# A decoder layer on one core: another bank and another sender for the first pair, feed-forward weights scaled by GpSimd, bounds in three operations

## The reference, cut to what matters

```python
x = layernorm(x + self_attention(x))          # q, k, v with biases, wo, bo
x = layernorm(x + cross_attention(ctx, ctx, x))  # 8x8 weights shared by all heads
x = layernorm(x + ffn(x))

def qlinear(x, W, b):            # ffn: qlinear, exact gelu, qlinear; 128 -> 512 -> 128
    amin, amax = min(x), max(x)                      # over the whole tensor
    scale = maximum((amax - amin) / 255, 1e-8)
    zp = clip(round(-amin / scale) - 128, -128, 127)
    xq = clip(round(x / scale) + zp, -128, 127)
    sw = maximum(max(abs(W)) / 127, 1e-8)
    wq = clip(round(W / sw), -127, 127)
    return ((xq - zp) @ wq.T) * (scale * sw) + b
```

## Time and profile before

| | us |
|---|---|
| median of 3 runs (lowest, highest) | 349.32 (348.51, 349.51) |
| the profiled execution, its own time | 350.94 |
| its span | 349.2 |
| busy: VectorE, TensorE, ScalarE, GpSimd | 309.9, 268.3, 251.3, 191.7 |
| mean granted clock of TensorE | 0.899 |

### The profile page before, as it was taken

How to read it: one execution, slowest core, us unless ns; L and a number is a source line. 1 busy time by engine, 2 the same in 40 slices (tenths; PEclk the granted TensorE clock), 3 DMA queues, 4 the chain that set the end, 5 groups by cost and what they waited for, 6 DMA issues and landing times.

```text
span 349.2 us, 12360 instructions
## 1 busy us (share of the span) xinstructions
PE 268.3 (77%) x4897; PEld 170.9 (49%) x4899; DVE 309.9 (89%) x708; ACT 251.3 (72%) x504; POOL 191.7 (55%) x393
## 2 busy tenths in 40 slices
PE   3678989799999999999999877898884276301991
PEld 2445656466666666666666544555552132000561
DVE  5756799899999999999999976999989579997794
ACT  2134788698988888888888874778782299902995
POOL 6233879857665766676667725665331018302285
PEclk9999999999999999999999996999996557655696
DMA  1352233232332333323423222332000000000035
GB/s 53 86 165 70 76 110 96 80 111 85 109 110 80 109 110 87 101 80 113 115 78 102 69 79 73 109 94 57 21 3 0 1 2 0 0 0 0 0 92 151
DMA packets 48992, 25.13 MB, mean 72 GB/s; under 512 B 6440, under 2 KB 48808, under 8 KB 48936
## 3 DMA queue, kind: packets, MB, share of 16 engines
q1 hardware_dynamic: 46936, 23.76, 23.7%
q10 hardware_dynamic: 2000, 0.59, 0.7%
HBM read 9.39 MB, written 2.10 MB: 33 GB/s over the span
## 4 chain that ended last, share of the span: by engine, by line
POOL 37%; issue 24%; DVE 19%; PE 9%; ACT 4%; DMA 3%; SPq 2%; POOLq 1%; ACTq 0%; DVEq 0%; another core or an unknown queue 0%
POOL rstd L561 7%; DVE h_ext L1023 5%; DVE h_ext L1024 5%; POOL arena_h L589 3%; POOL var_eps L558 3%; POOL parts_cq L394 3%; DVE neg_max L909 3%; POOL parts_cq L392 3%; POOL parts_ck L394 3%; POOL x_bias L578 2%; POOL parts_ck L392 2%; POOL parts_sq L394 2%; POOL parts_sk L394 2%; POOL parts_sq L392 2%; SPq L427 2%
## 5 line engine op out<-in xcount | busy, mean ns | idle before, releaser
L909 DVE TENSOR_REDUCE neg_max<-ps 128x8 f32<-128x1024 f32 x128 | 156.5, 1223 | 15.2 <-PE ps L1146 14.7
L721 ACT ACTIVATE probs<-ps 128x1024 f32<-128x1024 f32 x64 | 65.6, 1025 | 23.2 <-PE ps L1153 23.2
L712 ACT ACTIVATE probs<-ps 128x1024 f32<-128x1024 f32 x64 | 65.7, 1026 | 19.8 <-PE ps L1153 16.4
L1146 PE MATMUL ps<-arena_h 31*128 31x128 f16 x1024 | 53.5, 223 | 22.7 <-DVE neg_max L909 10.9
L1146 PEld LDWEIGHTS ps<-arena_h 31*128 31x128 f16 x1024 | 31.2, 95 | 57.7 <-DVE neg_max L909 39.7
L1153 PE MATMUL ps<-arena_h 32*128 32x128 f16 x1024 | 52.4, 220 | 0.7 <-ACT probs L721 0.6
L558 POOL TENSOR_TENSOR var_eps<-mean_var,eps_col 128x1 f32<-128x1 f32 x64 | 12.2, 191 | 66.0 <-DVE mean_var L893 66.0
L1174 PE MATMUL ps<-probs,arena_q 128*32 128x128 f32 x1024 | 42.5, 285 | 0.9 <-ACT u_sb L731 0.9
L1174 PE MATMUL ps<-probs,arena_h 128*32 128x128 f32 x1024 | 41.7, 281 | 0.0
L561 POOL TENSOR_TENSOR rstd<-var_eps,minus_half 128x1 f32<-128x1 f32 x64 | 35.2, 551 | 5.1 <-POOL var_eps L558 0.2
L1153 PEld LDWEIGHTS ps<-arena_h 32*128 32x128 f16 x1024 | 29.9, 94 | 1.7 <-ACT probs L721 1.0
(11 more groups left out here) (164 smaller groups left out, 622.6 us busy)
## 6 DMA issues: line engine op xcount, KB each, us to landing
arena_h<-parts_sq SPq DMA_DIRECT2D x48, 64.0 KB, 1.9
arena_h<-parts_ck SPq DMA_DIRECT2D x48, 64.0 KB, 2.3
arena_h<-parts_cq SPq DMA_DIRECT2D x48, 64.0 KB, 2.2
arena_h<-parts_sk SPq DMA_DIRECT2D x45, 64.0 KB, 2.0
xT_in<-in_xT_dram SPq DMA_DIRECT2D x16, 128.0 KB, 2.4
xN_in<-in_xN_dram SPq DMA_DIRECT2D x16, 128.0 KB, 2.4
cT_in<-in_cT_dram SPq DMA_DIRECT2D x16, 128.0 KB, 2.5
cN_in<-in_cN_dram SPq DMA_DIRECT2D x16, 128.0 KB, 2.3
```

The source lines that it names most:

```text
L712: act.activation(probs[1][:, :], ps_s2, ACT.Exp, scale=SCALE).then_inc(ex, 1)
L721: act.activation(probs[0][:, :], ps_s2, ACT.Exp, scale=SCALE).then_inc(ex, 1)
L909: dve.tensor_reduce(neg_max[b.par][:, HH * half:HH * half + HH], ps_s1.rearrange("p (h k) -> p h k", h=HH), AXX, ALU.max, negate=True).the ...
L1146: ins = pe.matmul(ps_s1[:, at:at + S], q[r:r + MAX_AT, j, :], kk[r:r + MAX_AT, j, :], start=True, stop=True, skip_group_check=True)
```

## The change

It touches many places:

- Pair 0: k goes to another PSUM bank (`k_sums`), its semaphore counts q and k apart, the product that turns the two biases (`turn_bqk`) runs between q's and k's; q's product waits for wq alone. SP sends the high terms of q, its low term and k's low term (`first_fill`), ScalarE k's two high terms, ahead of v's copies. Four of the setup loads go to ScalarE's queue at the start. GpSimd's first big clearing (L526) waits for k's split; VectorE clears only ring 1, GpSimd rings 2 and 3 in slot -2, and builds the blocks there; `setup_products` moves up within slot 0.
- Cross pairs: `cq_pairs` also holds back a pair until the slot after that in which the k of pair i-2 is sent (cq 12 from slot 48 to 49, cq 13 from 50 to 51); contexts are loaded one slot earlier; the fourth cross ring is cleared in slot 11.
- Weights: GpSimd scales them in slots 6 and 7 and makes them integers in slots 9 and 10.
- Bounds of the integers: from zero's rounding in three operations, LO = max(min(ZU, 0), -255), HI = LO + 255.
- x's third piece goes to GpSimd; ScalarE copies and makes words after gelu 2 of each group of 4, not 0 and 1.
- In slot 66 the layernorm of `outputs` comes last.
- TensorE does 10 and 8 products that nobody reads around `share_extremes(1)`.
- The last group's root: the addition on VectorE, the power on GpSimd in two halves.

```diff
-INVERSE_AT, X_SCALES, H_SCALES = 5, 12, 17
-DVE_PIECES = 3
+INVERSE_AT, X_SCALES, H_SCALES = 5, 11, 16
+DVE_PIECES = 2
-XT_AT, XN_AT, CT_AT, CN_AT = 8, 3, 8, 6
+XT_AT, XN_AT, CT_AT, CN_AT = 8, 3, 9, 6
-CROSS_RING_AT = (1, 3, 5, 7)
+CROSS_RING_AT = (1, 3, 5, 11)
+SCALE_AT, INTS_AT = (6, 7), (9, 10)
+SUM_AHEAD = TASKS + 2
@@ cq_pairs
-    return [i for i in range(PAIRS) if max(C_POS[2 * i] - CQ_AT, S_POS[2 * i] + X1_TURNED) == k]
+    free = [C_POS[2 * (i - 2)] - FILL_AT + 1 if i > 1 else FIRST_SLOT for i in range(PAIRS)]
+    return [i for i in range(PAIRS) if max(C_POS[2 * i] - CQ_AT, S_POS[2 * i] + X1_TURNED, free[i]) == k]
@@ sync
+        def k_sums(i):
+            return ps_u[:, 0:PAIR] if i == 0 else ps_p[:, PAIR:2 * PAIR]
+            def first_fill():
+                sp.wait_ge(split_hi["sq"], 1)
+                for t in (0, 1):
+                    sp.dma_start(stack["sq"][0][t::ROW_STEP, :, :],
+                                 parts["sq"][0][:, Q_PARTS[t], :]).then_inc(stacks_landed("sq", 0)[0], 16)
+                sp.wait_ge(split_done["sq"], 1)
+                sp.dma_start(stack["sq"][0][2::ROW_STEP, :, :], parts["sq"][0][:, Q_PARTS[2], :]).then_inc(stacks_landed("sq", 0)[0], 16)
+                sp.wait_ge(split_done["sk"], 1)
+                sp.dma_start(stack["sk"][0][1::ROW_STEP, :, :], parts["sk"][0][:, K_PARTS[1], :]).then_inc(stacks_landed("sk", 0)[0], 16)
@@ gpsimd
+            pool.wait_ge(split_done["sk"], 1)
             pool.memset(rest, 0.0).then_inc(v_zeroed, 1)
-                if k == -1:
+                if k == -2:
+                    pool.memset(arena_h[:, (RING + 2) * words:2 * RING * words], MROW_PAIR)
+                    pool.memset(arena_h[:, 2 * words:RING * words], 0.0).then_inc(rest_cleared, 1)
                     blocks()
+                if k in SCALE_AT:
+                    j = SCALE_AT.index(k)
+                    w = (w1_sb, w2_sb)[j]
+                    pool.wait_ge(w_step, 3)
+                    pool.tensor_scalar(w[:, :], w[:, :], w_inv[:, j:j + 1], MAGIC, ALU.mult, ALU.add).then_inc(w_magic, 1)
+                if k in INTS_AT:
+                    j = INTS_AT.index(k)
+                    pool.wait_ge(w_magic, j + 1)
+                    pool.tensor_scalar((w1_q, w2_q)[j][:, :], low_words((w1_sb, w2_sb)[j][:, :]), 127.0, -127.0,
+                                       ALU.min, ALU.max).then_inc(w_ints, 1)
...
-                pool.tensor_scalar(c(ZU), c(ZR), -MAGIC, -128.0, ALU.add, ALU.add).then_inc(q_step, 1)
+                pool.tensor_scalar(c(ZU), c(ZR), -1.0, MAGIC, ALU.mult, ALU.add).then_inc(q_step, 1)
-                pool.tensor_scalar(c(ZP), c(ZU), -128.0, 127.0, ALU.max, ALU.min).then_inc(q_step, 1)
+                pool.tensor_scalar(c(LO), c(ZU), 0.0, -255.0, ALU.min, ALU.max).then_inc(q_step, 1)
-                pool.tensor_scalar(c(LO), c(ZP), -1.0, -128.0, ALU.mult, ALU.add)
-                pool.tensor_scalar(c(HI), c(ZP), -1.0, 127.0, ALU.mult, ALU.add).then_inc(f_lh, 1)
+                pool.tensor_scalar(c(HI), c(LO), 1.0, 255.0, ALU.mult, ALU.add).then_inc(f_lh, 1)
@@ scalar
+            act.dma_start(wo_raw[:, :], woT_x).then_inc(w_cross, 16)
+            for j, w in enumerate((Wk, Wq, Wv)):
+                act.dma_start(small_w[:, j, :], w.unsqueeze(0).broadcast_to([H, E, E])).then_inc(w_cross, 16)
-                if k == 3:
-                    act.wait_ge(w_step, 3)
-                    for j, w in enumerate((w1_sb, w2_sb)):
-                        act.activation(w[:, :], w[:, :], ACT.Identity, bias=magic_col[:, :],
-                                       scale=w_inv[:, j:j + 1]).then_inc(w_magic, 1)
-                if hc == 1 and c == 0:
-                    x_to_words(3)
-                if hc == 0 and 1 <= c < NCH - 2:
+                if hc == 2 and c + 1 < NCH:
+                    xqT_out(c + 2)
+                if hc == 2 and c + 2 < NCH:
                     x_to_words(c + 3)
-                if hc == 1 and c + 1 < NCH:
-                    xqT_out(c + 2)
@@ vector
-                dve.memset(arena_h[:, RING * words + words:2 * RING * words], MROW_PAIR)
-                dve.memset(arena_h[:, words:RING * words], 0.0).then_inc(cleared, 1)
+                dve.memset(stack_words["sk"][1], MROW_PAIR)
+                dve.memset(stack_words["sq"][1], 0.0).then_inc(cleared, 1)
+            dve.wait_ge(f_ag, 4 * NG)
+            dve.tensor_scalar(o_root[g % 4][:, 0, :], o_mv[g % 4][:, :, 1], qs[1][:, EOUT:EOUT + 1], None,
+                              ALU.add).then_inc(f_le, 1)
@@ tensor
+                if k == 0:
+                    setup_products()
...
                 product(1)
                 if k < LEAD_SLOTS:
                     projections(k)
-                if k == 0:
-                    setup_products()
-                if hc == 1 and c < NCH - 1:
+                if hc == 2 and c < NCH - 1:
                     turn_x(c + 2)
+            def unread_products(count):
+                for _ in range(count):
+                    pe.matmul(bank(0), w1_q[:, 0:128], w2_q[:, :], start=True, stop=True)
             pe.wait_ge(f_g, NU + 1)
+            pe.wait_ge(f_xo, NP)
+            pe.wait_ge(f_mx, 2 * (NU + 1) - 6)
+            unread_products(10)
             share_extremes(1)
+            unread_products(8)
```

More of the change, by code:

```diff
@@ L960, in slot @@
                     mean_variance(x)
-                if k == 4:
-                    weight_ints()
+                if k == SUM_AHEAD:
+                    for t in outputs(k):
+                        new_x(t)
                 for i in EXT_SLOTS.get(k, ()):
@@ L1100, in _, with turn_bqk @@
         def _(pe):
[L1102 to L1107 removed]
+            def turn_bqk():
+                pe.wait_ge(columns, 1)
+                pe.wait_ge(w_b, 32)
+                for j in range(2):
+                    last = pe.matmul(ps_t[:, j:j + 1], bqk_row[0:1, j, :], one_cell[0:1, 0:1], start=True, stop=True,
+                                     skip_group_check=True)
+                last.then_inc(b_turned, 1)
             def setup_products():
```

88 lines of the change are left out of this document (46 added, 42 removed).

## The result

The changed kernel takes **337.69 us** (median of 4 runs, 336.97 to 339.59), the kernel before 349.19 (4 runs, 348.51 to 349.51): a ratio of 0.9681, 95% interval 0.9637 to 0.9726. Forecast were 337.3 us and a range of 334.5 to 343. The profiled execution has a span of 335.2 us and a time of 336.97, the lowest of its four; the one of before had a span of 349.2 and lay 1.8 above its median. So the stages of the two profiles differ by 14.0 us, the medians by 11.5.

What follows compares the result with a forecast made beforehand. VectorE's own work was taken to bound from 68 to 196 us, so gains lay elsewhere. Terms 3.0 + 1.25 + 0.5 + 4.1 + 0.3 + 0.35 + 1.05 + 1.5 = 12.05 off 349.32 gave 337.3 us, range 334.5 to 343.

Steps and rivals of the forecast that it cites:

- slots 5 to 14: Early attention slots: cq's split ends earlier without slot 7's clearing, less GpSimd's weight work and slot 11's clearing; net +0.5 us.
- hole: Slots 49 to 53: later cq 12 and 13 and earlier cT shorten GpSimd's landing wait; 4.1 of 5.8 us won.
- opening: Start to first scores: later memset, separate bank for k and earlier issues bring first scores to 12.0 from 13.86; 1.85 us.
- setup products: Slots 0 to 1: operands made earlier, products run while VectorE reduces, costing 0.65 there; 1.1 to 1.2 us won.
- weights: Weight scalings leave ScalarE (0.9) and conversions leave VectorE (0.35) for GpSimd; 1.25 us won, GpSimd's operations at 0.65 each.
- x's scale and first gelus: Behind attention: last mean earlier 0.3, bounds of x 0.35, x_ints on GpSimd and gelu 2 moved ahead 1.05 us.
- tail: End: unread products raise TensorE's clock, then ScalarE binds with seven normalisations of 1.59; 1.5 us won.
- (1): Rival: the landing wait moves with the split to slots 49 and 51, the hole keeping 4.8 of 5.8 us; chance 0.2.
- (2): Rival: GpSimd becomes the bound after slot 9, giving -2.4 us instead of +0.5; 340.2 us, chance 0.15.
- (3): Rival: unread products don't lift TensorE's clock, the tail wins only 0.3 us; 338.5 us, chance 0.12.
- (4): Rival: slower, TensorE's clock at its lower level through the attention, 0.4 us a slot; 40 slots give 353.3; chance 0.03.
- (5): Rival: nothing happens, early gains absorbed by a GpSimd-bound stretch and the hole stays; 349 us, chance 0.03.

Runs made afterwards that it cites:

- e2: Changed kernel with GpSimd's first memset (3072 words) put back at the front; 339.02 us, ratio 0.9696.
- e6: Changed kernel without its eighteen unread products around the second sharing of extremes; 339.38 us, ratio 0.969.
- e11: Changed kernel with cT loaded 8 slots ahead instead of 9, plus twelve more unread products around the first sharing of extremes; 334.53 us, ratio 0.9571.
- e3: Changed kernel with the blocks back in slot -1 and the setup products back at the end of slot 0; 340.61 us, ratio 0.9752.
- e7: Changed kernel with three x pieces rounded by VectorE and the old order of ScalarE and TensorE in the feed-forward; 339.48 us, ratio 0.9694.
- e12: Changed kernel with cross q 12 and 13 split in slots 50 and 52, plus twelve more unread products around the first sharing of extremes; 335.18 us, ratio 0.9569.
- e5: Changed kernel with the weights' scalings back on ScalarE in slot 3 and their roundings back on VectorE in slot 4; 339.51 us, ratio 0.9688.
- e9: Changed kernel with the first pair's k back in q's bank, so q's biased copy waits for both products; 338.1 us, ratio 0.965.
- e1: The changed kernel run again without edits; 338.14 us, ratio 0.9688.
- e8: Changed kernel with twelve more unread products, seven before and five after the first sharing of extremes; 338.2 us, ratio 0.9661.
- e4: Changed kernel with cross q 12 and 13 split and sent in their old slots, 48 and 50; 339.32 us, ratio 0.972.

## Why the prediction was right, step by step

By stages, the terms as forecast, as in the one profile of the changed kernel, and as in the mean of the profiled runs whose edits leave the stage alone (us won; without e2 and e6, and without e11, which moves a load in every slot, for slots 5 to 14 and the hole):

| stage | forecast | one profile | mean |
|---|---|---|---|
| opening (to the first maximum) | 1.85 | 1.85 | 1.82 |
| setup products (slots 0 to 1) | 1.15 | 2.23 | 1.95 |
| slots 1 to 3 | 0 | 1.46 | 0.98 |
| weights (slots 3 to 5) | 1.25 | 0.95 | 0.95 |
| slots 5 to 14 | +0.5 | -0.27 | -0.41 |
| slots 14 to 49 | 0 | -0.44 | -0.52 |
| hole (slots 49 to 55) | 4.1 | 3.21 | 2.90 |
| x's scale and first gelus | 1.70 | 2.04 | 2.04 |
| tail (from ext) | 1.5 | 2.98 | 2.81 |
| slots 55 to 61 | 0 | -0.01 | -0.06 |
| sum | 12.05 | 14.0 | 12.5 |

**The opening** came out as worked out, time by time. What the sum didn't say is that its parts don't add: undoing the memset loses 1.87, the bank 1.03, the sending 2.03, together 4.9 for a gain of 1.85. They stand in one chain, and each is worth its price only with the others in place.

**Slots 0 to 1.** The mechanism was right (e3 gives back the 5.69 of before, to 0.01), the size not: I had let the block products cost 0.65 inside the reduction and kept some of the rest; they cost next to nothing there.

**Slots 1 to 3** I had at nothing. From rows on both sides: the 16 products on the probabilities take 1.08 us in slot 1 of the kernel before and 0.64 in the changed one (timelines; the PEclk column is 1.00 in both there and doesn't tell them apart).

```profile
28.41 1.08 PE L1174 MATMUL ps<-probs,arena_q 128*32 128x128 f32 x16
```

```profile
24.34 0.64 PE L1216 MATMUL ps<-probs,arena_q 128*32 128x128 f32 x16
```

I read the factor of 1.7 as TensorE's two levels, 1.2 and 2.4 GHz, since L1386 differs by 1.8 where the clock column does tell them apart (e6). Where these products are at 1.08 in slot 1 (before, e3, e7, e12), slots 1 to 3 take 10.6 to 10.9 us, else 9.1 to 9.6. As e7 and e12 have the same opening as the changed kernel, the edits don't decide it alone: it is a gain that most runs get, 1.0 in the mean.

**Weights.** GpSimd's price as bounded; ScalarE's blocking of the exp is the 0.9 that I read in the earlier trace rows. The 0.35 for VectorE's conversions wasn't there: they lay in a wait (e5's 0.94).

**Slots 5 to 14.** The step that failed: I laid cq 0's late landing on GpSimd's ring clearing alone. In the kernel before that fits: the split of cq 0 ends at 62.13 and its fill goes at 62.16. In the changed kernel the clearing is gone and the split ends at 54.59, 0.8 us ahead of slot 9, but the fill goes at 55.44, when SP has sent the fill of ck (52.63 to 55.40), and the row maximum of slot 10 still waits 1.52. So SP's queue is what binds next. That cT's load, which this very change put there, is what makes the fill late is not shown: e9 and e12 are in time with it. In e1, e5 and e8 the slot behind the late landing lasts 1.3 us longer too, at a granted clock of 0.64; whether it comes from the wait isn't shown, since the changed kernel's profile has the wait and keeps 1.00. The half microsecond for the clearing in slot 11 was right.

**The hole.** The wait was read rightly and is shown from three sides: old slots, 8.9; one later, 3.4 to 5.2; two later, none. The size was 1.2 too large, and two things were missing: slots 53 to 55 take a further 1.2 or 2.5 us in half of the profiles, those in which the granted clock falls there (e1), and in e11 no gain from cT's earlier load is seen. What the wait costs is less clear: e12, without it, saves 3.0 us against e8, but e4, with nearly all of it back, loses only 1.8 of the 3.8 that slots 49 to 53 won in the mean, and 0.8 of the 2.9 of slots 49 to 55. Where the rest is from stays open, as there is one profile of before.

**x's scale and the first gelus** were within 0.35 in sum: up to the first x_ints 0.90 was won where 0.65 was forecast, behind it 1.14 where 1.05 was (e7 gives back 0.78 of it).

**Tail.** The term was mis-sized by half, 1.5 against 2.8. ScalarE did bind, as the text said, but seven groups of 1.59 was wrong: 28 normalisations take 10.03 us, 1.43 a group, since the pauses of 0.93 in all and a part of each one's length were themselves TensorE's. e6 puts 1.35 of the 2.8 on the unread products. The rest fits the halved last group (VectorE waits 1.00 for it and not 1.79) and the shorter bounds (0.35 and not 0.65), but these weren't tried singly. Of the rivals, (1) would have kept 4.8 us of the hole (slots 49 to 55 keep 2.6 of the 5.8 in the changed profile); (2) holds in its sign for slots 5 to 14, but by SP's queue and at a third of its size; (3) is out (e6), (4) never showed: the clock is 1.00 from 68 to 196, and (5) is out by 11 us. Two of my own signs of being wrong did appear: slots 11 and 12 last 3.72 and 3.79 us, and slots 49 to 53 still lose 1.5, where VectorE waits 1.08 us for a root at 212.83. The bounds were added wrongly: the upper ones give 16.7, so 332.6 and not 330.5. And 0.3% was too fine for what a measurement tells: runs of the changed kernel lie 0.8% apart, and the ratio is known to 0.45%.

**Why the total fits.** Too little in the setup, the clock, x's scale and the tail (3.4 by the means) was balanced by too much in the hole, the slots 5 to 49 and the weights (3.0): part of the closeness is luck. The terms were read from an execution of 350.94 us but taken from the median of 349.32: the means' 12.5 from 350.94 give 338.4, against the medians of 337.69 and 338.14. The single profile's 14.0 is 1.5 more than a usual run wins.

## What to carry to other kernels

A stage's duration between two marks that every kernel has (here a reduction in each slot) shows an edit of 0.3 us where whole times scatter by 4: compare stages, and know each stage's scatter before one profile of it is believed. Edits in one chain aren't worth the sum of their single prices; and a microsecond won or lost early can be gone behind the next landing (e9 is 1.04 behind e1 at the first slot and level with it at slot 10). When an engine is cleared of work ahead of a transfer, look at once at the queue that sends it: here GpSimd was in time and SP's queue was not. When a load is moved to an earlier slot, ask what it stands in front of; e11 wins 3.7 us against e8 by moving one back. And look at the granted clock before a stage's scatter is laid on its landings.
